# Attention's output turned by VectorE and two passes through DRAM while the FFN runs, in place of TensorE's transposes in the last stage

## The reference, cut to what matters

```python
xn = layernorm(x)
s  = gated_delta_attention(xn)     # 16 heads of 128: o = rmsnorm(o) * norm_weight * silu(z); s = o.reshape(T, 2048) @ W_out
g  = silu(ffn(xn))                 # top 2 of 8 experts, 512 -> 2048 -> 512, gelu, weighted by the router
out = x + s * g
```

## Time and profile before

| | |
|---|---|
| median of 3 runs | 2127.39 us (2127.2 to 2128.92) |
| profiled execution | 2126.86 us, its span 2125.1 us |
| TensorE busy | 2046.0 us, 96% of the span |
| VectorE / ScalarE / GpSimd busy | 61% / 43% / 39% |
| DMA | 150.68 MB, mean 71 GB/s |

### The profile page before, as it was taken

One profiled execution on the slowest core, in us unless ns is written; L12 is line 12 of the kernel. 1 busy time (PEld: TensorE's weight loads), 2 busy tenths in 40 slices (PEclk: granted clock), 3 DMA queues, 4 the chain that ended last, 5 costly groups with the idle time before them and its releaser, 6 DMA issues.

```text
span 2125.1 us, 39639 instructions
## 1 busy us (share of the span) xinstructions
PE 2046.0 (96%) x13986; PEld 1737.0 (82%) x13986; DVE 1297.4 (61%) x3105; ACT 907.5 (43%) x2525; POOL 826.1 (39%) x2123
## 2 busy tenths in 40 slices
PE   5689999999999999999999999999999999999999
PEld 3578888888888888888888778888888888887887
DVE  6768887778778887878776354444444443364222
ACT  4456555455555565555655432222222322232111
POOL 2356666565666666666657210011001110010001
PEclk8889999999999999999999999999999999999999
DMA  4233544444535435343443220000000111022331
GB/s 130 40 74 76 96 87 99 74 97 81 90 90 94 93 81 98 81 103 81 98 78 86 70 80 20 21 31 21 30 20 21 40 31 49 0 89 91 119 119 60
DMA packets 219060, 150.68 MB, mean 71 GB/s; under 512 B 113264, under 2 KB 200176, under 8 KB 216816
## 3 DMA queue, kind: packets, MB, share of 16 engines
q1 hardware_dynamic: 185680, 144.15, 29.0%
q10 hardware_dynamic: 33184, 4.01, 1.2%
HBM read 118.48 MB, written 29.62 MB: 70 GB/s over the span
## 4 chain that ended last, share of the span: by engine, by line
PE 68%; issue 12%; DVE 6%; DMA 5%; POOL 4%; ACT 3%; SPq 2%; ACTq 0%; POOLq 0%; DVEq 0%
PE bank L317 17%; PE bank L319 16%; PE bank L318 16%; DMA VT<-v_dram 4%; PE bank L549 2%; PE bank L558 2%; PE bank L532 2%; PE bank L452 2%; PE bank L540 2%; PE bank L568 2%; PE bank L511 1%; POOL V L1760 1%; PE bank L517 1%; POOL prod L1758 1%; POOL y_out L1809 1%
## 5 line engine op out<-in xcount | busy, mean ns | idle before, releaser
L1758 POOL TENSOR_TENSOR prod<-A_in,V 128x60 f32<-128x60 f32 (+24 forms) x992 | 301.0, 303 | 273.3 <-DMA A_in<-a_dram 203.0
L1760 POOL TENSOR_TENSOR V<-V,prod 128x60 f32<-128x60 f32 (+24 forms) x992 | 310.9, 313 | 77.7
L1097 ACT ACTIVATE hid<-bank,bias 128x512 f32<-128x512 f32 x128 | 88.2, 689 | 458.0 <-PE bank L319 458.0
L1562 DVE TENSOR_TENSOR h_lo<-hid,h_hi 128x512 fp32r<-128x512 f32 x128 | 89.9, 704 | 314.3 <-ACT h_hi L1104 314.1
L1799 POOL TENSOR_TENSOR ffn_w_lo<-ffn_raw,ffn_w_hi 128x1024 fp32r<-128x1024 f32 x32 | 77.7, 2429 | 479.5 <-ACT ffn_w_hi L1087 479.5
L1576 DVE SCALAR_TENSOR_TENSOR gate_acc<-bank,rw,gate_acc 128x512 f32<-128x512 f32 x240 | 177.8, 748 | 63.0 <-PE bank L319 61.3
L317 PE MATMUL bank<-ffn_w_hi,h_hi 128*128 128x512 f32 x512 | 201.0, 393 | 2.7 <-DVE gate_acc L1571 1.6
L317 PE MATMUL bank<-xn_hi,ffn_w_hi 128*128 128x512 f32 x512 | 202.1, 395 | 0.0
L319 PE MATMUL bank<-xn_hi,ffn_w_lo 128*128 128x512 f32 x512 | 201.1, 393 | 0.0
L319 PE MATMUL bank<-ffn_w_hi,h_lo 128*128 128x512 f32 x512 | 200.9, 392 | 0.0
L318 PE MATMUL bank<-xn_lo,ffn_w_hi 128*128 128x512 f32 x512 | 200.9, 392 | 0.0
(11 more groups left out here) (225 smaller groups left out, 5167.1 us busy)
## 6 DMA issues: line engine op xcount, KB each, us to landing
E<-eg_dram SPq DMA_DIRECT2D x64, 256.0 KB, 7.8
A_in<-a_dram SPq DMA_DIRECT2D x32, 512.0 KB, 4.0
decb<-dec_dram SPq DMA_DIRECT2D x128, 128.0 KB, 4.0
og_dram<-og SPq DMA_DIRECT2D x64, 256.0 KB, 2.1
ffn_raw<-w SPq DMA_DIRECT2D x32, 512.0 KB, 3.6
og_in<-og_dram SPq DMA_DIRECT2D x16, 1024.0 KB, 5.3
w_raw<-group_w SPq DMA_DIRECT2D x48, 256.0 KB, 7.6
x_in<-x SPq DMA_DIRECT2D x8, 512.0 KB, 6.4
```

What stands on the lines that cost most here:

```text
L1097: act.activation(hid[:, i % 2, :], bank[i % 4][:, :], ACT.Gelu_apprx_tanh, bias=bias1[:, k, f * NF + ft:f * NF + ft + 1]).then_inc(S_["gel ...
L1562: dve.tensor_tensor(h_lo[:, hb, ft, :], hid[:, i % 2, :], h_hi[:, hb, ft, :].bitcast(f32), SUB).then_inc(S_["h_lo"], 1)
L1758: pool.tensor_tensor(prod[:, 0:m, 0:n], column, V[:, vb, 0:m, j:j + 1].to_broadcast([P, m, n]), MUL).then_inc(S_["product"], 1)
L1760: pool.tensor_tensor(V[:, vb, 0:m, j + 1:B32], V[:, vb, 0:m, j + 1:B32], prod[:, 0:m, 0:n], ADD).then_inc(S_["solve_step"], 1)
```

## The change

The output of attention is turned during the FFN, unit by unit. A unit `u` is 512 tokens by the 128 features of one head; there are 64.

- `load_swap(u)`: four loads from `og_dram`, one for each group of 32 features. Each brings 16 blocks of 32 tokens by 32 features, with the token within its block on the partition: 512 runs of 128 bytes a load, 2048 a unit. Before it, from the third unit on, SyncE waits for VectorE to be done with unit u-2.
- `swap_og(u)`: one VectorE transpose of 32x32 blocks, 128x512, from `og_x` to `og_y`. Now the feature is on the partition and the token along the row.
- `store_swap(u)`: one store into a new DRAM tensor `ogT_dram`, 512 runs of 512 bytes.

VectorE does five units in each of the parts 1 to 12 and four in part 13, after the sums of a block: one each behind the first three blocks and two behind the fourth. SyncE loads units 0 and 1 before `load_ffn(1, 1)`; the rest of its issues stand between the weight loads. In the last stage `load_og(t)` reads `ogT_dram` (1 MB, rows of 8 KB), `turn_og` is gone, ScalarE and VectorE read `og_in` instead of PSUM, and `load_og` waits for VectorE's `ogT_lo` where it waited for TensorE. `load_og(0)` moves from the head of the FFN to behind the last unit. `og_x` and `og_y` lie where `og_in0` does.

```diff
+NSWAP = NSB * HEADS
+SWAPS = 5
...
+        ogT_dram = nc.dram_tensor("ogT_dram", (NT, P, HEADS, P), f32, kind="Internal").ap()
...
+        swap = ExitStack()
+        og_x = alloc(swap, "og_x", [2, 4 * P])
+        og_y = alloc(swap, "og_y", [2, 4 * P])
+        swap.close()
         og_in = [alloc(top, "og_in0", [HEADS * HD])]
...
+        def swaps(n):
+            return range(max(SWAPS * (n - 1), 0), min(SWAPS * n, NSWAP))
...
-            def turn_og(t):
-                for m in range(4):
-                    i = 4 * t + m
-                    if m == 0:
-                        pe.wait_ge(S_[f"og_in{t % OG_BUFS}"], 16 * (t // OG_BUFS + 1))
-                    if i >= 4:
-                        pe.wait_ge(S_["ogT_lo"], i - 3)
-                    else:
-                        pe.wait_ge(S_["gelu"], NBLK * NF - 3 + m)
-                    for h in range(4):
-                        r = pe.transpose(bank[m][:, h * P:(h + 1) * P], og_in[t % OG_BUFS][:, (4 * m + h) * P:(4 * m + h + 1) * P], C["ident"])
-                    r.then_inc(S_["turned"], 1)
...
-                else:
-                    turn_og(0)
                 down(j)
             for t in range(NT):
-                if t + 1 < NT:
-                    turn_og(t + 1)
                 finish(t)
...
-                    act.wait_ge(S_["turned"], 4 * t + m + 1)
+                    if m == 0:
+                        act.wait_ge(S_[f"og_in{t % OG_BUFS}"], 16 * (t // OG_BUFS + 1))
...
-                    act.copy(ogT_hi[:, tb, 4 * m:4 * m + 4, :], bank[m][:, :].rearrange("p (h t) -> p h t", h=4)).then_inc(S_["ogT_hi"], 1)
+                    act.copy(ogT_hi[:, tb, 4 * m:4 * m + 4, :], og_part(t, m)).then_inc(S_["ogT_hi"], 1)
...
+            def swap_og(u):
+                dve.wait_ge(S_[f"og_raw{u % 2}"], 64 * (u // 2 + 1))
+                if u >= 2:
+                    dve.wait_ge(S_[f"og_turned{u % 2}"], 16 * (u // 2))
+                dve.transpose(og_y[:, u % 2, :], og_x[:, u % 2, :]).then_inc(S_["og_swap"], 1)
...
                 down(j)
+                if n:
+                    for u in swaps(n):
+                        if u % SWAPS == sb or (u % SWAPS == NSB and sb == NSB - 1):
+                            swap_og(u)
...
+            def load_swap(u):
+                t0, e = u // HEADS * SB, u % HEADS
+                if u >= 2:
+                    sp.wait_ge(S_["og_swap"], u - 1)
+                for q in range(NQD):
+                    at = e * P + q * B32
+                    src = og_dram[t0:t0 + SB, at:at + B32].rearrange("(b i) j -> i b j", i=B32)
+                    dst = og_x[q * B32:(q + 1) * B32, u % 2, :].rearrange("p (b j) -> p b j", j=B32)
+                    sp.dma_start(dst, src).then_inc(S_[f"og_raw{u % 2}"], 16)
+
+            def store_swap(u):
+                sp.wait_ge(S_["og_swap"], u + 1)
+                t, e = u // HEADS * CPS, u % HEADS
+                dst = ogT_dram[t:t + CPS, :, e, :].rearrange("t p c -> p t c")
+                sp.dma_start(dst, og_y[:, u % 2, :].rearrange("p (t c) -> p t c", t=CPS)).then_inc(S_[f"og_turned{u % 2}"], 16)
...
             def load_og(t):
                 if t >= OG_BUFS:
-                    sp.wait_ge(S_["turned"], 4 * (t - OG_BUFS + 1))
+                    sp.wait_ge(S_["ogT_lo"], 4 * (t - OG_BUFS + 1))
...
+            load_swap(0)
+            load_swap(1)
             for n in range(1, len(FPARTS)):
                 load_ffn(n, 1, index)
+                for u in swaps(n - 2):
+                    if u % SWAPS == 0:
+                        store_swap(u)
+                        if u + 2 < NSWAP:
+                            load_swap(u + 2)
                 load_ffn(n, 2, index)
                 if n == 2:
                     load_out(0)
-                    load_og(0)
...
+                for u in swaps(n - 2):
+                    if u % SWAPS:
+                        store_swap(u)
+                        if u + 2 < NSWAP:
+                            load_swap(u + 2)
+            load_og(0)
             load_out(3)
```

More of the change, by code:

```diff
@@ L72 @@
 x0 x1 x2 x3 x4 x5 x6 x7 constants constants1 small_weights gate_in w_raw0 w_raw1 og_out0 og_out1
-ffn_bias ffn_bias1 ffn_raw0 ffn_raw1 wo_raw og_in0 og_in1 og_in2 x_res0 x_res1 out0 out1
+ffn_bias ffn_bias1 ffn_raw0 ffn_raw1 wo_raw og_raw0 og_raw1 og_turned0 og_turned1 og_in0 og_in1 og_in2 x_res0 x_res1 out0 out1
 rows_out eg0 eg1 dec0 dec1 begin0 begin1 a_out a_in v_out vt_in
@@ L82 @@
 up_hi gelu ffn_hi gate_tanh wo_hi ogT_hi
-h_lo acc0 acc gate wo_scaled ogT_lo gated
+h_lo acc0 acc gate wo_scaled ogT_lo gated og_swap
 ffn_lo wo_lo out_sum
-up down turned s_sum
+up down s_sum
 """.split()
@@ L252, in fw_rows, with og_part @@
             return fw[m, part, n % 2][:, :].rearrange("p (k n) -> p k n", k=ND if m == 1 else NF)
+        def swaps(n):
+            return range(max(SWAPS * (n - 1), 0), min(SWAPS * n, NSWAP))
+        def og_part(t, m):
+            return og_in[t % OG_BUFS][:, 4 * m * P:4 * (m + 1) * P].rearrange("p (h t) -> p h t", h=4)
         def bc_heads(v):
@@ L1596, in turned_og @@
                     dve.wait_ge(S_["ogT_hi"], 4 * t + m + 1)
-                    dve.tensor_tensor(ogT_lo[:, tb, hs, :], bank[m][:, :].rearrange("p (h t) -> p h t", h=4), ogT_hi[:, tb, hs, :].bitcast(f32), SUB).then_inc(S_["ogT_lo"], 1)
+                    dve.tensor_tensor(ogT_lo[:, tb, hs, :], og_part(t, m), ogT_hi[:, tb, hs, :].bitcast(f32), SUB).then_inc(S_["ogT_lo"], 1)
+            def swap_og(u):
[3 more added lines that the diff above has]
+                dve.transpose(og_y[:, u % 2, :], og_x[:, u % 2, :]).then_inc(S_["og_swap"], 1)
             def finish(t):
@@ L1990, in load_out @@
                 sp.dma_start(wo_raw[:, :, :], w_out[hs.start * HD:hs.stop * HD, :].rearrange("(a p) n -> p a n", p=P)).then_inc(S_["wo_raw"], 16)
+            def load_swap(u):
[12 more added lines that the diff above has]
+                sp.dma_start(dst, og_y[:, u % 2, :].rearrange("p (t c) -> p t c", t=CPS)).then_inc(S_[f"og_turned{u % 2}"], 16)
             def load_og(t):
                 if t >= OG_BUFS:
-                    sp.wait_ge(S_["turned"], 4 * (t - OG_BUFS + 1))
+                    sp.wait_ge(S_["ogT_lo"], 4 * (t - OG_BUFS + 1))
                 elif t:
                     sp.wait_ge(S_["up"], NBLK * NF)
-                sp.dma_start(og_in[t % OG_BUFS][:, :], og_dram[t * P:(t + 1) * P, :]).then_inc(S_[f"og_in{t % OG_BUFS}"], 16)
+                else:
+                    sp.wait_ge(S_["og_turned0"], 16 * (NSWAP // 2))
+                    sp.wait_ge(S_["og_turned1"], 16 * (NSWAP // 2))
+                    sp.wait_ge(S_["og_swap"], NSWAP)
+                sp.dma_start(og_in[t % OG_BUFS][:, :], ogT_dram[t, :, :, :].rearrange("p e c -> p (e c)")).then_inc(S_[f"og_in{t % OG_BUFS}"], 16)
             def load_x(t):
```

## The result

The changed kernel took 2111.91 us (median of 4 executions, 2104.49 to 2114.96), the kernel before 2127.3: a ratio of 0.9916, 95% interval 0.9891 to 0.9941. The forecast was 2110 us, with a range of 2104 to 2120. The profiled execution is the fastest of the four, 2104.49 us with a span of 2102.7.

The account below looks back on a forecast made before the run. TensorE was taken to bound the FFN and last stage. Against the profiled 2126.86 us, -24.8 + 5.5 + 1.7 + 0.5 = -17.1 gave 2109.8; with the median 0.5 above that execution, 2110 us, range 2104 to 2120.

Parts of the forecast that it names:

- The transposes: Last stage: 14 sets of TensorE transposes go, 1.77 us each, 24.8 us saved.
- Rival D: Last stage: another engine sets the tile's pace, so the change frees nothing; 2134 us, chance 0.03.
- The delay at the head: FFN's head: eight short-run loads ahead of part 1's weights delay them 5.5 us, between 3.6 and 7.9.
- The clock at the head: FFN's head: TensorE's longer pause brings a low clock behind it, 1.7 us lost (0 to 3.4).
- The first tile: Last stage's start: finish(0) waits for the last block's sum, then meets the low clock; 0.5 us lost (0 to 2.2).
- The FFN: Inside the FFN: the added transposes, loads and stores stay hidden behind TensorE; cost 0.
- A: FFN's head: loads cost only their issue, 3.6 us, and the clock holds; 2106 us, chance 0.15.
- B: FFN's head: a short run costs what a 1 KB run does, 13.2 us, low clock twice as long; 2119 us, chance 0.15.
- C: Head and FFN: slow reads at 76 runs per us, 54 us at the head alone, 2158 us; chance 0.06.

Follow-up runs that it names:

- long_head: Changed kernel with the first eight loads at the FFN's head reading 32 rows of 2 KB instead of 512 runs of 128 bytes; ratio 0.9904.
- both_bias: The kernel of both, with the three bias and norm-weight loads behind part 1's weights as well; ratio 0.9831 to the kernel before.
- both: Changed kernel with the edits of late and tail_early together; ratio 0.9844 to the kernel before.
- finer: Changed kernel with each load of a unit cut in two: 64-byte runs, twice the runs and issues; one execution, 2114.66 us.
- tail_early: Changed kernel with the first two turned tiles split earlier and finish() in PSUM banks 0 and 1 instead of 4 and 5; ratio 0.9874.
- late: Changed kernel with the first two units loaded behind part 1's weights instead of ahead of them; ratio 0.9886 to the kernel before.

## Why the prediction was right, step by step

That the median, 2111.91 us, came within 2 us of 2110 is partly luck. The sum of the terms missed by 2.6 us (19.7 us gained behind the last store, 17.1 forecast), and attention, which the forecast did not touch, moves single executions by some 10 us. What the profiles bear out is the mechanism, term by term, with one term mis-sized.

**The transposes, 24.8 us: right.** From finish(1)'s first matmul to the last of all, 186.07 us before and 162.97 after: 13 sets gone, 1.78 each. With the fourteenth, 1.66 from 1932.35 to finish(1), it is 24.8. Rival D is out: no engine took over the tile's pace.

**The delay at the head, 5.5 us: the term that was mis-sized; 2.7 measured**, below even the lower bound of 3.6. That bound took the weights' landing, 5.80 us, as fixed. It was not. The two bias loads, issued 2.3 us ahead of the weights, were still moving before (they land after 3.8 us), and the 4.6 us of extra issue time (4.78 from the first exchange load to the weights, against 0.2 without) partly ran while those drained. The landing fell to 3.97, which gave back 1.8: 4.6 - 1.8 = 2.8. In the prediction's words, "each us that this load is late is a us of the kernel" held; what failed is that its issue being late by x makes it late by x. That the issues and not the runs set the delay was bounded correctly, and long_head showed it (3.60 us of issue with long runs, 4.60 with short). TensorE's pause came to 4.36 us, not 7, and ScalarE's wait to 12.09, not 15, for the same reason. That the bias loads were what the weights had waited for fits both_bias, whose wait fell below the kernel before's by 2.5 us, 0.5 of it by an earlier issue. It fits the landings too: 4.80 to 7.01 us in the four kernels that issue the weights right behind the bias loads, 3.57 to 5.05 where exchange loads stand between. In the changed kernel the bias loads landed after 4.2 us, at about 1215, ahead of the weights' issue at 1217.34. But single landings vary by a us or two, so the 1.8 us are well supported and not proven.

**The clock at the head, 1.7 us: right.** 0.79 over 8 us loses 1.7, of which some lay in the pause itself; TensorE's own way from the pause to the last block lengthened by 1.4. It was worked out for a pause of 7 us, but the cost hardly depended on the pause: 1.4 to 1.6 us behind pauses of 2.84 (both), 3.87 (long_head) and 8.29 us (finer), with tail_early's 2.6 behind 5.30 the exception.

**The first tile, 0.5 us: the mechanism right, the size too small, 1.0.** The pause came to 7.68 us and was ended by the sum, both as said. Its low clock lasted longer than the one before (0.57 over 1916 to 1928): finish(0) took 13.2 us, 2.3 above 10.88, where I had 1.7 with a bound of twice that. That is nearly the whole miss; finish(0) began where the prediction had it, 1920.1 once the head's 4.1 us and the shorter attention are taken out.

**The FFN, 0: right.** One transpose took 0.70 us (between 0.55 and 0.87 as bounded), the loads landed in 2.7 us, no wait on `og_x`:

```profile
L1600 DVE STREAM_TRANSPOSE og_y<-og_x x64: 667/701/705, 1271.1 to 1831.7; 128x512 f32<-128x512 f32 x64
...
DMA to landing us min/median/max: 2.2/2.7/4.5
```

The sum: -24.8 + 2.7 + 1.4 + 1.0 = -19.7, as measured behind the last store; -17.1 was forecast. The head was put 2.8 us too high and its clock 0.3, the first tile 0.5 too low.

**The rivals.** A came nearer than the forecast by the profiles: its sum is -24.8 + 3.6 + 0.5 = -20.7, 1.0 from the measured -19.7, where mine is 2.6 away. It named the head's cost best in kind (issues alone), but the clock did not hold, and its 3.6 us was too high as well. B is out: it had 13.2 us at the head, and at its 310 runs per us finer's units of 4096 runs would take 13.2 us, longer than the block of 10.9 that two units in five have, yet VectorE waited once, for 0.4 us. C (slow reads) is out with it, by a wide margin. Its figure was misread besides: the 78 GB/s of the earlier trace rows is a stretch in which the DMA engines were busy 0.23 of the time, so it is no limit of such reads, and the bias loads, broadcast reads too, landed 256 KB each in 3.8 us.

**Left open**: why attention takes 1210 us in one execution and 1222 in another, in both kernels, and what makes the landing of part 1's weights vary by one to two us. The change touches neither.

## What to carry to other kernels

Work moved off the engine that bounds a stage is worth what it took between two starts there, and a block transpose plus two passes through DRAM can pay for it when DMA and VectorE idle beside a long stage. Look at the seams, not at the bulk: 131,072 short reads behind TensorE's back cost nothing, eight issues ahead of the one load that everybody waited for cost 4 us, and moving them two lines down got 3.4 to 4.4 us back. And when a load's issue is delayed, ask what it was queued behind: part of the delay may be time it would have spent waiting anyway.

## What the runs showed of the hardware that I had not expected

Where VectorE now takes both operands of its subtraction from SBUF (L1594), it and GpSimd's addition hold each other up. With one operand in PSUM they overlapped as well (in one tile the addition ran from 1971.29 and the subtractions from 1971.58), and the subtraction's longest was 692 ns and the addition's median 1288; now they are 1789 and 1775 (changed kernel, VectorE, then GpSimd; min/median/max):

```profile
L1594 DVE TENSOR_TENSOR ogT_lo<-og_in,ogT_hi x64: 677/682/1789, 1918.3 to 2080.0; 128x512 fp32r<-128x512 f32 x64
...
L1816 POOL TENSOR_TENSOR y_out<-y_out,x_res x16: 1262/1775/1779, 1935.7 to 2098.9; 128x512 f32<-128x512 f32 x16
```

In one tile the first subtraction started at 1957.42 and took its usual 692 ns, the addition started at 1957.48 and took 1.78 us, and the second subtraction, from 1958.0, took 1789 ns: it ended 0.5 us behind the addition. VectorE's work over a tile rose from 3.2 to 4.05 us for it, hidden here under 10.88. In both_bias, where such a subtraction meets GpSimd's 4.6 us one (1902.63 to 1907.27), it took 4686 ns.

And a load of 512 runs of 128 bytes costs SyncE's queue 0.575 us from issue to issue when eight come in a row (0.54 to 0.59 in the other runs with them at the head), one of 32 runs of 2 KB 0.45. The price depends on what is ahead in the queue: right behind part 1's weights the same eight took 0.87 us each in late and 1.12 in both.
